# An adaLN block on eight cores: layer-norm stage moved ahead of two modulation groups, row DMAs on ScalarE's queue, unpacking interleaved with the second layer norm

## The reference

```python
mod = (silu(c) @ wmod).reshape(6, 1, 1024)        # c: 1024 values, wmod: 1024 x 6144
sa, ca, ga, sb, cb, gb = mod
ga = sign(ga) * maximum(abs(ga), 0.25)            # gb likewise
h = layernorm(x) * (1 + ca) + sa
q, k, v = h @ Wq.T + bq, h @ Wk.T + bk, h @ Wv.T + bv
sim = q @ k.T + rel_emb[bucket] * 0.125 + causal  # per head, bucket of the distance i - j
x = x + ga * (softmax(sim) @ v @ Wo.T + bo)
h = layernorm(x) * (1 + cb) + sb
s = 127 / max(abs(h), over the row)
x = x + gb * ((clip(round(h * s), -128, 127) / s) @ w + bias)   # w: ternary, unpacked from 2-bit codes
```

## Time and profile before

| | us |
|---|---|
| time of the kernel before, median of 2 runs (1336.41 and 1339.66) | 1338.03 |
| the profiled execution, its own time | 1336.04 |
| its span on the slowest core (core 7) | 1334.4 |
| spans of the eight cores | 1326.6 to 1334.4 |
| stage 1, from the start to the first matmul L610 | 314.2 |
| stage 2, to the last VectorE pass L794 | about 713.6 |
| stage 3, from there to the end | about 306.5 |
| busy: TensorE, VectorE, ScalarE, GpSimd | 768.5, 546.8, 409.7, 127.0 |

### The profile page before, as it was taken

How to read it: one execution, slowest core, us unless ns; L and a number is a source line. 1 busy time by engine, 2 the same in 40 slices (tenths; PEclk the granted TensorE clock), 3 DMA queues, 4 the chain that set the end, 5 groups by cost and what they waited for, 6 DMA issues and landing times.

```text
span 1334.4 us, 16687 instructions; the slowest of 8 cores (1326.6 to 1334.4 us)
## 1 busy us (share of the span) xinstructions
PE 768.5 (58%) x3869; PEld 314.9 (24%) x3869; DVE 546.8 (41%) x1364; ACT 409.7 (31%) x785; POOL 127.0 (10%) x262
## 2 busy tenths in 40 slices
PE   0334210545888788878878887888598000111198
PEld 0000000212443333333334333332132000000043
DVE  0000117663324343342433334243465286655567
ACT  0000100320573636546354654637100002222200
POOL 0101122100111212111121210000000000000000
PEclk9999999999898797878889888888799555555589
DMA  9667321231101102011110110000000100000023
GB/s 293 190 211 253 86 47 16 30 44 35 13 10 27 14 9 30 7 29 13 25 14 9 28 10 17 1 17 2 16 1 1 32 0 0 1 0 1 0 99 154
DMA packets 45653, 59.57 MB, mean 45 GB/s; under 512 B 33149, under 2 KB 36301, under 8 KB 42488
## 3 DMA queue, kind: packets, MB, share of 16 engines
q0 software_dynamic: 32352, 33.59, 12.2%
q1 hardware_dynamic: 13208, 24.93, 5.8%
HBM read 56.74 MB, written 10.14 MB: 50 GB/s over the span
## 4 chain that ended last, share of the span: by engine, by line
PE 52%; DVE 21%; DMA 12%; issue 9%; ACT 4%; DVEq 1%; SPq 1%; POOL 0%; ACTq 0%; POOLq 0%
PE p_o L718 15%; PE p_s L610 8%; PE p_s L679 7%; PE p_v L638 5%; DMA swm<-wm 5%; PE p_s L781 4%; PE p_f L918 4%; DMA sx<-x 2%; DVE soT L588 2%; PE p_mod L374 2%; DVE shT L447 2%; DVE stats6b L267 2%; DMA srowb<-dtaus 2%; PE p_v L644 2%; PE p_tr L444 2%
## 5 line engine op out<-in xcount | busy, mean ns | idle before, releaser
L694 ACT ACTIVATE sPt<-p_s 128x512 bf16<-128x512 f32 (+3 forms) x640 | 297.3, 534 | 246.3 <-PE p_s L679 244.2
L718 PE MATMUL p_o<-sPt,sv 128*65 128x512 bf16 (+3 forms) x640 | 229.7, 408 | 94.2 <-DVE soT L752 37.0
L906 PE MATMUL p_tr<-sid,sy 128*128 128x128 bf16 x128 | 25.9, 270 | 203.1 <-DVE sy L901 186.2
L649 DVE CAST sv<-p_v 128x128 bf16<-128x128 f32 x128 | 37.7, 295 | 234.5 <-PE p_v L644 232.9
L679 PE MATMUL p_s<-sqt,skt 64*128 64x512 bf16 (+3 forms) x640 | 126.0, 405 | 7.4 <-DVE skt L617 7.4
L718 PEld LDWEIGHTS p_o<-sPt,sv 128*65 128x65 bf16 x640 | 66.4, 117 | 220.2 <-issue 211.6
L638 PE MATMUL p_v<-swv,shT 128*128 128x128 bf16 x1024 | 85.4, 231 | 0.0
L702 DVE TENSOR_TENSOR sPt<-sPt,sE 128x240 bf16<-128x240 bf16 (+1 forms) x256 | 60.9, 265 | 38.6 <-ACT sPt L694 34.6
L638 PEld LDWEIGHTS p_v<-swv,shT 128*128 128x128 bf16 x1024 | 72.0, 104 | 15.4 <-issue 8.1
L374 PE MATMUL p_mod<-swm,scsil 128*1 128x512 f32 x96 | 44.4, 619 | 53.0 <-DMA swm<-wm 52.4
L781 PE MATMUL p_s<-swo,soT 128*128 128x512 bf16 x256 | 62.1, 386 | 15.8 <-DVE soT L588 15.8
(11 more groups left out here) (103 smaller groups left out, 797.0 us busy)
## 6 DMA issues: line engine op xcount, KB each, us to landing
swm<-wm POOLq DMA_DIRECT2D x24, 1024.0 KB, 5.9
sx<-x SPq DMA_DIRECT2D x16, 512.0 KB
out<-sx SPq DMA_DIRECT2D x16, 512.0 KB
srbt<-dsumB SPq DMA_DIRECT2D x16, 256.0 KB
swq<-wq POOLq DMA_DIRECT2D x64, 32.0 KB, 2.1
swk<-wk POOLq DMA_DIRECT2D x64, 32.0 KB, 2.1
swv<-wv POOLq DMA_DIRECT2D x64, 32.0 KB, 2.1
swo<-wo POOLq DMA_DIRECT2D x8, 256.0 KB, 3.7
```

The costliest lines, as they stand in the source:

```text
L694: hb=hb: e.activation(sPt[:, sl, hb, qoff:512], pb[:, qoff:512], AF.Exp, bias=EXPB, scale=F1),
L718: sl=sl, nkt=nkt, vb=vb: e.matmul(p_o2[hb][:, qoff:512], sv[:, vb, kt, 65 * hb:65 * hb + 65], sPt[:, sl, hb, qoff:512], start=(kt == 0), s ...
L906: sq.add("tensor", lambda e, b=b, c=c, pp=pp: e.transpose(p_tr3[pp][:], sy3[:, b, 128 * c:128 * (c + 1)], sid128[:]), reads=[f"sy:{b}", "s ...
```

## The change

The line numbers in this section are those of the kernel before unless they stand in a fence of the changed one.

- The bias factors' small part (matmul, Exp, `dtaus`) moves to the front, ahead of the modulation. The bias loop over the 16 heads moves behind modulation group 2.
- The modulation is now `mod_group(jg)`. Group 0 stays in front. Groups 1 and 2 move behind the layer norm's statistics, transposes and copies.
- `wload(0)` and `wload(1)` move from behind all modulation groups to behind group 0.
- The row stores and row loads of stage 1 (`drows`, `s16`, `load_row`, `save_row`, the load of `fbr`) are issued by ScalarE instead of SyncE, and the barrier waits for ScalarE's DMAs too.
- In stage 3 the unpacking of chunk c moves from ahead of the statistics to behind the copies of tile t = c, and its multiplication by `gbw` moves from VectorE to GpSimd.
- `skap` moves from GpSimd to VectorE, and every other copy out of the transposes (even c) from VectorE to ScalarE.

```diff
-    BARRIER_DMA = ("sync",)
+    BARRIER_DMA = ("sync", "scalar")
...
+            sq.add("tensor", lambda e: e.matmul(p_gen[0:16, 0:128], srel[:], soh[:],
+                                                start=True, stop=True),
+                   reads=["rel", "oh"], writes=["p_gen"])
...
+            sq.add("sync", lambda e: e.dma_start(out=dtaus[:], in_=staub[:]),
+                   reads=["taub"], writes=["dtaus"], dma=True)
...
-            for jg in range(3):
+            def mod_group(jg):
                 for c in range(NCH):
                     p = (NCH * jg + c) % 2
                     sq.add("gpsimd", lambda e, jg=jg, c=c, p=p: e.dma_start(
...
-                    sq.add("sync", lambda e, jg=jg, sl=sl: e.dma_start(
+                    sq.add("scalar", lambda e, jg=jg, sl=sl: e.dma_start(
                         out=drows[:, 2048 * jg + 512 * sl:2048 * jg + 512 * (sl + 1)],
                         in_=srowst[0:1, sl % 2, :]),
...
+            mod_group(0)
+            sq.add("scalar", lambda e: e.dma_start(
+                out=s16[:],
+                in_=drows[:, 0:2048].rearrange("o (r j) -> (o r) j", j=128)),
+                reads=DR[0:4], writes=["s16"], dma=True)
...
+            wload(0)
+            wload(1)
 
             for t in range(NT):
                 ln_stats(t)
...
+            mod_group(1)
+            mod_group(2)
+
+            for h in range(NH):
+                sq.add("sync", lambda e, h=h: e.dma_start(
+                    out=srowb[:, 0:384], in_=dtaus[h:h + 1, :]),
+                    reads=["dtaus"], writes=["srowb"], dma=True)
...
             def load_row(offs, deps):
-                sq.add("sync", lambda e, offs=offs: e.dma_start(
+                sq.add("scalar", lambda e, offs=offs: e.dma_start(
...
             def save_row(slot):
-                sq.add("sync", lambda e, slot=slot: e.dma_start(
+                sq.add("scalar", lambda e, slot=slot: e.dma_start(
...
-            for c in range(NCH):
+            def unpack_chunk(c):
                 for s in range(4):
                     sq.add("vector", lambda e, c=c, s=s: e.tensor_scalar(
                         sei[:], spk[:, c, :], 2 * s, 3,
...
-                sq.add("vector", lambda e, c=c: e.tensor_mul(
+                sq.add("gpsimd", lambda e, c=c: e.tensor_mul(
                     swf[:, c, :], swf[:, c, :], gbw[:]),
-                    reads=["gbw"], writes=[f"swf:{c}"])
+                    reads=["gbw", f"swf:{c}"], writes=[f"swf:{c}"])
...
-                sq.add("gpsimd", lambda e, t=t, b=b: e.tensor_scalar(
+                sq.add("vector", lambda e, t=t, b=b: e.tensor_scalar(
                     skap[:, t:t + 1], stmp1[:, b:b + 1], s_swb[:], 1.0 / 127.0,
...
-                    sq.add("vector", lambda e, t=t, c=c, pp=pp: e.tensor_copy(
-                        shT[:, c, 128 * t:128 * (t + 1)], p_tr3[pp][:]),
-                        reads=[f"ptr:{pp}"], writes=[f"hT:{c}:{t // 4}"])
+                    eng = "scalar" if c % 2 == 0 else "vector"
+                    if eng == "scalar":
+                        sq.add("scalar", lambda e, t=t, c=c, pp=pp: e.activation(
+                            shT[:, c, 128 * t:128 * (t + 1)], p_tr3[pp][:],
+                            AF.Identity, bias=F0, scale=F1),
+                            reads=[f"ptr:{pp}"], writes=[f"hT:{c}:{t // 4}"])
...
+                if t < NCH:
+                    unpack_chunk(t)
```

More of the change, by code:

```diff
@@ L256, in build_nc @@
             sems[f"c:{e}"] = ctx.enter_context(nc.semaphore(f"c_{e}"))
-        for e in ("sync", "gpsimd"):
+        for e in ("sync", "gpsimd", "scalar"):
             for k in range(Sched.NDMA):
@@ L390, in build_nc @@
                     DR.append(f"dr:{jg}:{sl}")
[L392 to L412, removed]
@@ new lines, in build_nc @@
+            sq.add("scalar", lambda e: e.dma_start(
+                out=s16[:],
+                in_=drows[:, 0:2048].rearrange("o (r j) -> (o r) j", j=128)),
+                reads=DR[0:4], writes=["s16"], dma=True)
+            sq.add("tensor", lambda e: e.transpose(p_c16[:], s16[:], sidf[:]),
+                   reads=["s16", "idf"], writes=["p_c16"])
+            sq.add("vector", lambda e: e.tensor_copy(a1c[:], p_c16[:]),
+                   reads=["p_c16"], writes=["a1c"])
+            sq.add("vector", lambda e: e.tensor_scalar_add(
+                a1c[:, 8:16], a1c[:, 8:16], 1.0),
+                reads=["a1c"], writes=["a1c"])
@@ new lines, in wload @@
+            def wload(d):
+                wb = d % 2
+                for wname, wt, stile in (("wq", wq, swq), ("wk", wk, swk),
+                                         ("wv", wv, swv)):
+                    for c in range(NCH):
+                        sq.add("gpsimd", lambda e, wt=wt, stile=stile, d=d,
+                               wb=wb, c=c: e.dma_start(
+                                   out=stile[:, wb, c, :],
+                                   in_=wt[128 * c:128 * (c + 1),
+                                          128 * d:128 * (d + 1)]),
+                               writes=[f"{wname}:{wb}"], dma=True)
@@ L451, in build_nc @@
                         reads=[f"ptr:{pp}", "a1c"], writes=[f"hT:{c}:{t // 4}"])
+            mod_group(1)
[4 more added lines that the diff above has]
+                    reads=["dtaus"], writes=["srowb"], dma=True)
+                sq.add("tensor", lambda e: e.matmul(
+                    p_gen[:, 0:384], ones1[:], srowb[:, 0:384], start=True, stop=True),
+                    reads=["srowb", "ones1"], writes=["p_gen"])
+                sq.add("vector", lambda e: e.tensor_copy(srep[:], p_gen[:, 0:384]),
+                       reads=["p_gen"], writes=["srep"])
+                sq.add("sync", lambda e, h=h: e.dma_start(
+                    out=dtau[:, 384 * h:384 * (h + 1)], in_=srep[:]),
+                    reads=["srep"], writes=[f"dtau:{h}"], dma=True)
             def load_row(offs, deps):
-                sq.add("sync", lambda e, offs=offs: e.dma_start(
+                sq.add("scalar", lambda e, offs=offs: e.dma_start(
                     out=srow[:], in_=drows[:, offs:offs + D]),
@@ L513, in build_nc @@
             save_row(3)
[L516 to L519, removed]
-                    for c in range(NCH):
-                        sq.add("gpsimd", lambda e, wt=wt, stile=stile, d=d,
-                               wb=wb, c=c: e.dma_start(
-                                   out=stile[:, wb, c, :],
-                                   in_=wt[128 * c:128 * (c + 1),
-                                          128 * d:128 * (d + 1)]),
-                               writes=[f"{wname}:{wb}"], dma=True)
-            wload(0)
-            wload(1)
             for c in range(NCH):
```

28 lines of the change are left out of this document (18 added, 10 removed).

## The result

| | before, us | after, us |
|---|---|---|
| median of the runs | 1337.77 (1335.89 to 1343.09) | 1354.30 (1351.82 to 1405.24) |
| ratio, 95% interval | | 1.011 [1.0094, 1.0125] |
| start to first matmul of stage 2 | 310.5 | 337 |
| stage 2 | 712.4 | 708 to 727 |
| last VectorE pass of stage 2 to the end | 307 | 298.0 |

Three of the eleven runs of the changed kernel fell in a slower state of the chip (1387 to 1405 us) which the ratio leaves out: without them its median is 1352.5 us, and the kernel is slower by 1.1%, 14.8 us. The lower rows are medians over the eight cores of the profiled executions, since the one of the changed kernel took 1364.98, 10.7 above its median, and its cores differ in stage 2, which the change leaves alone. By stages: +26.5 in stage 1, -9 in stage 3, together +17.5. That is nearly 3 us more than the 14.8 of the runs, and where these went stays open.

The account below looks back on a forecast made before the run. It took stage 1 as three latency-bound pieces in a row and VectorE as pacing stage 3; +14.3 for stage 1 and -6.9 for stage 3 gave +7.4, 1345.4 against 1338.03 us, range 1322 to 1365.

Parts of the forecast that it names:

- The weight pieces in front of `wm` make stage 1 serial: Stage 1: the ninth `wm` load waits 117.9 us of weight pieces, layer norm hidden; stage 2 starts 14.3 us later.
- 13 steps ... 4.02 each; now there are 15: Stage 1, `wm` chunks on TensorE: 15 steps at the old pace take 60.3 us, the modulation ending at 250.8.
- I take 2 us over the loop: Stage 1, bias loop: `wo` loads beside it add 0 to 1 us in about 10 turns, 2 us taken.
- The 2 us for ScalarE's queue: Stage 1, row tail: the second gate's row load stands behind the two passes writing `gat`, adding 2 us.
- Copies: Stage 3, transposes: copies on two engines do not shorten the turn and add 3.2 us; from below, a 10 us gain.
- `skap`, 0.27 each: Stage 3, each tile: `skap` on VectorE between GpSimd's bound and the reciprocal adds 0.27 us, 4.3 over 16.
- I take that row itself, 1.2: Stage 3: GpSimd's multiplication costs VectorE's chain 1.2 us per chunk, 9.6 for eight; bounds 0 and 2.4 per chunk.
- The unpacking, 3.2 a chunk: Stage 3: unpacking without its multiplication comes back into the tiles at 3.2 us for each of eight chunks, 25.6.
- That VectorE stands still for the product: Rival, stage 3: VectorE is held 2.3 us for each of eight GpSimd products, giving 1354 us; chance 0.22.
- That the product is free: Rival, stage 3: GpSimd's product does not delay VectorE, stage 3 gives -16.5 and the time is 1336; chance 0.20.
- The tiles' chain: Rival, stage 3: GpSimd's next bound queues behind its product, slower by over 2%, 1376 us at 5 us each; chance 0.09.
- Quick weight pieces: Rival, stage 1: pieces at 1.2 us, not 2.46, start stage 2 7 us earlier; 1314 us with free product; chance 0.05.

Follow-up runs that it names:

- own_tags: The changed kernel with a tag of its own for each weight piece; 1332.45 us, 0.9983 of the kernel before.
- weights_behind: The changed kernel with the 48 weight pieces issued behind modulation groups 1 and 2; 1352.2 us, 1.0137 of the kernel before.
- wo_later: The changed kernel with the eight `wo` loads moved behind the weight pieces of attention's first pass; 1342.85 us, 1.006 of the kernel before.
- before_own_tags: The kernel before with a tag for each weight piece and nothing else changed; 1346.93 us, 1.0083 of the kernel before.
- copies_vector: The changed kernel with all copies out of the second stage's transposes back on VectorE; 1343.95 us, 1.0055 of the kernel before.
- the interleaved one: Changed kernel reworked: bias head and `wm` chunk after each layer norm tile, pieces last, stage 3 engines as before; 1230.56 us with own tags, 1300.73 with shared.
- product_vector: The changed kernel with the unpacked chunk's product by `gbw` back on VectorE; 1344.31 us, 1.0069 of the kernel before.

## Why the prediction was wrong

The forecast was 1345, +7.4 us and no change that a measurement could tell; it came to 1354.3 in the median of all runs, +16.5, and +14.8 by the ratio, and this was told from no change. The mechanism was right: stage 1 becomes serial and loses, stage 3 gains. Terms of the sum were mis-sized, above all the pace of the chunks and the bias loop beside `wo`. Step by step:

- **The weight pieces in front of `wm` make stage 1 serial: right.** Their 117.9 us measured 118.4, the layer norm was done at 165.4 in the median of the cores (forecast 170) and TensorE idled before the ninth chunk.
- **"13 steps ... 4.02 each; now there are 15": too small.** The last matmul of the modulation moved by 252.9 - 140.3 = 112.6 us (medians); forecast was 248.9 - 142.29 = 106.6. That is 6.0 us more, most of it the pace of 4.22 to 4.38 over the 15 steps. On core 7, from which the forecast was worked out, the pace alone makes 5.3, and the 7.2 us from load to matmul came out as they stand. In own_tags and weights_behind, where two chunks had landed before TensorE asked for them, the last 13 steps took 4.05 and 4.00 us (medians). Why the chunks land in pairs otherwise was not tried.
- **"I take 2 us over the loop" for `wo`: the step that failed most.** The small DMA was priced at 0 to 1 us in ten turns; seven turns beside `wo` took (282.07 - 251.03) / 7 = 4.43 us each, the next eight (307.11 - 282.07) / 8 = 3.13, so it cost 1.3 us in each of seven, and the loop grew by 8.5. Both wo_later and before_own_tags show that cause. The price was guessed with no row behind it, though the trace before has such a row; it is shown below.
- **The 2 us for ScalarE's queue: right in kind, too large.** It costs 1.3, as the clamps show above; the tail took 24.6 against 25.5 forecast. Together 6.0 + 6.5 - 0.9 = 11.6, which takes +14.3 to +25.9 of the measured +26.5.
- **Statistics in the wait for `spk`: right,** 58.3 us against 58.0. **`ln_apply`: right,** seven waits of up to 1.15 are 7.9 against 8.4. **Copies: right,** a pair takes 0.79 against 0.74, though all that copies_vector has left for them is 1.7 us of the 3.2.
- **`skap`, 0.27 each: too large.** It starts 0.13 ahead of the reciprocal, 2.1 us in all instead of 4.3.
- **"I take that row itself, 1.2" for GpSimd's product: too small.** The add is stretched from 0.69 to 2.42, 1.73 us in each of eight tiles, 13.8 instead of 9.6. The bound of 2.4 us for each chunk was not reached. The nearest row was float32 on one partition and VectorE's, a poor stand-in. The Trainium skill (SBUF, section "SBUF: two separate sides") had said that the two exclude each other for a whole instruction, and the trace agrees: the add ends 0.55 us behind the product (1089.91 and 1089.36), and the product takes 2.42 us. The multiply L876, which had started first, kept its 0.68. The estimate from its GPSIMD Engine Reference (section "3.1 Elementwise — side-by-side cycle accounting") was 2.2.
- **The unpacking, 3.2 a chunk: a little too large.** A tile with it and with GpSimd's product takes 14.52 us. The one tile with the product and without it takes 12.74, of which 1.15 are the wait for `ln_apply` that the unpacking hides. So it costs 14.52 - 11.59 = 2.93, 23.4 us in all instead of 25.6. The terms as read here add up to -58.3 + 23.4 + 2.1 + 3.2 + 7.9 + 13.8 = -7.9 for stage 3; it measured -9, and the last microsecond is open.

**The row that was overlooked.** In the kernel before, the row stores of group 0, 2 KB each, run beside `wm` loads. SyncE on core 7, the four stores and the load that waits for the last of them:

```profile
71.37 2.61 SPq L386 DMA_DIRECT2D drows<-srowst  x4
78.43 0.31 SPq L393 DMA_DIRECT2D s<-drows  x1
```

The last store was issued at 73.8, so 4.7 us passed; the median of the cores is 2.9. In the changed kernel, with weight pieces beside it and on ScalarE's queue, it is 1.2 on every core. In weights_behind, on the same queue but with the `wm` loads there again, the median is 2.4. That is 1.2 to 1.7 us more for one small DMA beside large loads, and each of the loop's seven turns paid 1.3.

**The rivals.** That VectorE stands still for the product had given 1354. Its mechanism held and its number met the result, but by chance: it lays the whole error on stage 3, which came out 2 us better than forecast, and none of the 11.6 us missing in stage 1 is in it. That the product is free fell. The tiles' chain did not become the loss: 13.8 of its 49 us are held by GpSimd. Quick weight pieces were not in this kernel, but own_tags made them, and stage 2 then began at 310.8 on the median core, where it had begun before (310.5) and not 7 us earlier: the loop, at 57 us, took the rest.

The range rested on +10 to +24 for stage 1. It measured +26.5 there, outside. The time stayed inside because the upper end also took +3 for stage 3, which came to -9: two errors that met, and no merit of the range. Its lower bound has a slip besides: the -26 of stage 3 counts the copies' loss of 3.2 and their gain of 10 together; with the gain alone it is -29.7, and the lower end 1318.

## What to carry to other kernels

Before a serial run of loads is moved ahead of something, look at what serialises it (here one tag for eight DMAs) and at everything behind it in its queue: with the pieces moved behind the chunks, attention waited for them by the 32 us that stage 1 had gained. Own tags took 17 us off the changed kernel and 70 off the interleaved one, and cost the kernel before 11. Stretches that are bound by latency gain when they are interleaved, not when they are put in another order: here stage 2 starts 88 us earlier than before (222.2 against 310.5, medians), and with the 28 us of stage 3 the time falls by 8.7%. A loop that goes through a small DMA in each turn must be priced by who else is loading at that time.

## What the runs showed of the hardware

- A load of 768 bytes in a loop is waited for 2.65 us in the median with no large load beside it, and 4.0 us (3.2 to 4.8) beside loads of 128x1024 that are issued about 4.5 us apart (waits over all cores of the changed kernel). Loads made faster elsewhere can therefore cost time: before_own_tags, +0.8%.
- A weight piece of 128x128 takes 2.46 us when each waits for the one before, and one goes out each 27 / 48 = 0.56 us when they don't.
- A 128x1024 bf16 product takes GpSimd 2.42 us where VectorE takes 0.69, and holds VectorE's two-input add until it ends (2.42 us instead of 0.69 in each of eight tiles; 0.69 again in product_vector). The first 0.44 of the 2.42 lie beside VectorE's multiply, so no run shows the product alone.
